# Four PSUM banks for the first feed-forward product, and a W2 ternary loop on DVE with four load buffers and two result buffers

## What is computed

```
def bitlinear(x, W, b):
    w_scale = jnp.clip(jnp.mean(jnp.abs(W)), EPS, None)
    Wq = _ste(W, jnp.clip(jnp.round(W / w_scale), -1.0, 1.0) * w_scale)
    x_scale = jnp.clip(jnp.max(jnp.abs(x), axis=-1, keepdims=True), EPS, None)
    xq = _ste(x, jnp.clip(jnp.round(x * (QB / x_scale)), -QB - 1.0, QB) * (x_scale / QB))
    return jnp.einsum('bnd,hd->bnh', xq, Wq) + b
h = bitlinear(x, W1, b1)          # 1024 -> 4096
h = jax.nn.gelu(h, approximate=False)
return bitlinear(h, W2, b2)       # 4096 -> 1024
```

## Time and profile before

| | |
|---|---|
| median of three runs | 3119.3 us |
| profiled execution, its own time | 3135.53 us |
| its span, slowest core (core 1) | 3133.9 us |
| spans of the eight cores | 3091.9 to 3133.9 us |
| busy PE, DVE, ACT, POOL | 986.5, 1412.7, 579.8, 253.8 us |
| mean granted TensorE clock | 0.65 of 2.4 GHz |

### The profile page before, as it was taken

One profiled execution on the slowest core, in us unless ns is written; L12 is line 12 of the kernel. 1 busy time (PEld: TensorE's weight loads), 2 busy tenths in 40 slices (PEclk: granted clock), 3 DMA queues, 4 the chain that ended last, 5 costly groups with the idle time before them and its releaser, 6 DMA issues.

```text
span 3133.9 us, 14949 instructions; the slowest of 8 cores (3091.9 to 3133.9 us)
## 1 busy us (share of the span) xinstructions
PE 986.5 (31%) x3428; PEld 350.8 (11%) x3428; DVE 1412.7 (45%) x1172; ACT 579.8 (19%) x476; POOL 253.8 (8%) x196
## 2 busy tenths in 40 slices
PE   2752334633321000766662001101001010126644
PEld 0100111211100000222221000000000000002211
DVE  1000324345345677445543225676676767740011
ACT  0213224324432110222221002010101011000000
POOL 0000000000000000222222440000000000000000
PEclk9875667766665555777776555555555555559878
DMA  6754010100000000222212441101101010138766
GB/s 232 273 183 159 14 40 21 41 20 20 20 27 0 0 0 8 86 74 80 75 60 88 121 120 54 67 34 47 54 33 67 34 67 34 47 114 285 257 215 215
DMA packets 70696, 265.47 MB, mean 85 GB/s; under 512 B 7504, under 2 KB 7888, under 8 KB 64208
## 3 DMA queue, kind: packets, MB, share of 16 engines
q1 hardware_dynamic: 35744, 155.20, 14.4%
q0 software_dynamic: 18304, 67.12, 6.1%
q10 hardware_dynamic: 16560, 42.19, 4.2%
HBM read 214.15 MB, written 50.33 MB: 84 GB/s over the span
## 4 chain that ended last, share of the span: by engine, by line
DVE 41%; DMA 19%; PE 18%; ACT 10%; issue 7%; POOL 3%; DVEq 1%; SPq 1%; ACTq 1%; POOLq 0%
DVE X L100 17%; DVE Hh L100 10%; DVE SC L100 8%; DMA RB<-w2qsp 6%; PE PB L1066 6%; PE PB L734 5%; ACT SC L100 3%; DMA SC<-w2T 3%; PE PB L1265 2%; ACT X L100 2%; PE PB L1305 2%; POOL X L100 2%; DMA M<-w2qsp 2%; DVE M L100 2%; DMA w2qsp<-X 2%
## 5 line engine op out<-in xcount | busy, mean ns | idle before, releaser
L100 DVE TENSOR_TENSOR SC<-PB,BS 128x512 f32<-128x512 f32 x160 | 110.7, 692 | 432.2 <-PE PB L1305 243.5
L734 PE MATMUL PB<-Hh,WSB 128*128 128x512 bf16 x768 | 194.6, 421 | 243.6 <-POOLq L56 130.8
L1066 PE MATMUL PB<-Hh,W1Q 128*128 128x512 bf16 x512 | 150.1, 462 | 289.9 <-POOLq L56 223.4
L100 DVE TENSOR_TENSOR X<-X 128x2048 bf16<-128x2048 bf16 (+1 forms) x120 | 206.8, 1723 | 14.8 <-PE PB L527 1.6
L1265 PE MATMUL PB<-Hh,M 128*128 128x512 bf16 x128 | 47.3, 550 | 396.1 <-DVEq L56 396.1
L1066 PE MATMUL PB<-Hh,RB 128*128 128x512 bf16 x512 | 144.1, 448 | 68.7 <-DVEq L56 68.7
L100 ACT ACTIVATE X<-X 128x4096 bf16<-128x4096 bf16 (+1 forms) x24 | 73.1, 3048 | 493.4 <-DVEq L56 492.4
L1265 PE MATMUL PB<-X,RB 128*128 128x512 bf16 x128 | 47.4, 551 | 368.9 <-DVEq L56 368.9
L100 DVE TENSOR_SCALAR X<-X 128x2048 bf16<-128x2048 bf16 (+1 forms) x145 | 139.0, 959 | 53.3 <-ACTq L56 35.7
L100 ACT ACTIVATE X<-SC,CPF 128x512 bf16<-128x512 f32 x128 | 92.4, 722 | 328.7 <-DVEq L56 328.2
L1305 PE MATMUL PB<-X,M 128*128 128x512 bf16 x384 | 97.7, 403 | 115.8 <-DMA M<-w2qsp 115.6
(11 more groups left out here) (168 smaller groups left out, 1571.6 us busy)
## 6 DMA issues: line engine op xcount, KB each, us to landing
X<-h1qsp SPq DMA_DIRECT2D x96, 512.0 KB, 6.4
SC<-w1T POOLq DMA_DIRECT2D x32, 512.0 KB, 7.4
WSTG<-w1T SPq DMA_DIRECT2D x32, 512.0 KB, 4.0
h1sp<-X POOLq DMA_DIRECT2D x32, 512.0 KB, 3.0
WSTG<-w2T SPq DMA_DIRECT2D x8, 2048.0 KB, 9.1
WSTG<-wmodT SPq DMA_DIRECT2D x6, 2048.0 KB, 9.5
SC<-wmodT SPq DMA_DIRECT2D x12, 1024.0 KB, 8.9
M<-w2qsp ACTq DMA_DIRECT2D x48, 256.0 KB, 7.3
```

What stands on the lines that cost most here:

```text
L100: ins = f(*a, **k)
L734: E.matmul(PB[pp + gi][:, :], WSB[:, gi * 1024 + k * 128: gi * 1024 + (k + 1) * 128], ntile(Hh, k, j), start=(k == 0), stop=(k == KC - 1)),
L1066: E.matmul(PB[jp][:, :], w1q[hc % 4][:, k * 128:(k + 1) * 128], ntile(Hh, k, j), start=(k == 0), stop=(k == KC - 1)),
```

## The change

Two edits. In the first feed-forward product the bank becomes `(hc * NNT + j) % 4`, and a product waits for the eviction four back. The W2 stretch is written anew: 16 units of half a slice, four load buffers with a semaphore each, comparisons into the bf16 tiles `W1Q` and `RB`, the subtraction on DVE, and the result in one of two halves of `X[:, 4096:12288]`, of which slice `s` takes the half that slice `s - 2` had, after waiting for that write. The write stays on POOL's queue and goes by turns on two semaphores.

```diff
--- before.py
+++ after.py
@@ -1052,7 +1052,7 @@
         if hc + 2 < HC:
             emit_tern(hc + 2)
         for j in range(NNT):
-            jp = j % 2
+            jp = (hc * NNT + j) % 4
             gidx = hc * NNT + j
             for k in range(KC):
                 wv = []
@@ -1060,8 +1060,8 @@
                     wv = [tern_dvs[hc]]
                     if gidx == 0:
                         wv += [("sDV", xq_done)]
-                    if gidx >= 2:
-                        wv += [("sDV", ffn1_evacs[gidx - 2])]
+                    if gidx >= 4:
+                        wv += [("sDV", ffn1_evacs[gidx - 4])]
                 p.on("tensor", lambda E, hc=hc, j=j, k=k, jp=jp:
                      E.matmul(PB[jp][:, :],
                               w1q[hc % 4][:, k * 128:(k + 1) * 128],
@@ -1113,40 +1113,47 @@
         inc=("sDV", 1))
     pl_m1h = ("sDV", p.cnt["sDV"])
 
-    w2stage = WSTG[:, 0:4096]
-    for s in range(KC):
-        wv = [("sSPa", p.cnt["sSPa"]), ("sSPb", p.cnt["sSPb"])] if s == 0 \
-            else [("sDV", p.cnt["sDV"])]
-        p.on("sync", lambda E, s=s: E.dma_start(out=w2stage, in_=w2T[s]),
-             wait=wv, inc=("sW2", 16))
-        w2n = p.cnt["sW2"]
-
-        def tern2a(E, s=s):
-            E.tensor_scalar(SC[1][:, 0:2048], w2stage[:, 0:2048],
-                            WS2i[:, 0:1], 0.5, ALU.mult, ALU.is_ge)
-            return E.tensor_scalar(SC[2][:, 0:2048], w2stage[:, 0:2048],
-                                   WS2n[:, 0:1], 0.5, ALU.mult, ALU.is_ge)
-        p.on("vector", tern2a,
-             wait=[("sW2", w2n)] + ([("sSP", p.cnt["sSP"])] if s >= 1 else []),
-             inc=("sDV", 1))
-        p.on("gpsimd", lambda E: E.tensor_tensor(
-            TRN2A, SC[1][:, 0:2048], SC[2][:, 0:2048], ALU.subtract),
-            wait=[("sDV", p.cnt["sDV"])], inc=("sPL", 1))
-
-        def tern2b(E, s=s):
-            E.tensor_scalar(SC[1][:, 0:2048], w2stage[:, 2048:4096],
-                            WS2i[:, 0:1], 0.5, ALU.mult, ALU.is_ge)
-            return E.tensor_scalar(SC[2][:, 0:2048], w2stage[:, 2048:4096],
-                                   WS2n[:, 0:1], 0.5, ALU.mult, ALU.is_ge)
-        p.on("vector", tern2b, wait=[("sPL", p.cnt["sPL"])], inc=("sDV", 1))
-        p.on("gpsimd", lambda E: E.tensor_tensor(
-            TRN2B, SC[1][:, 0:2048], SC[2][:, 0:2048], ALU.subtract),
-            wait=[("sDV", p.cnt["sDV"])], inc=("sPL", 1))
-        dvn = ("sPL", p.cnt["sPL"])
-        p.on("gpsimd", lambda E, s=s: E.dma_start(
-            out=w2qsp[:, :, s * 128:(s + 1) * 128].rearrange("k p c -> p k c"),
-            in_=X[:, 4096:8192].rearrange("p (k c) -> p k c", k=HC)),
-            wait=[dvn], inc=("sSP", 16), dma=True)
+    w2stg4 = [SC[1][:], SC[2][:], SC[3][:], WSTG[:, 0:2048]]
+    w2sem4 = ["sW2", "sW2b", "sW2c", "sW2d"]
+    w2u_dv = {}
+    w2spl = {}
+    for u in range(2 * KC):
+        s, h = u // 2, u % 2
+        st = u % 4
+        if u < 4:
+            wv = [("sSPa", p.cnt["sSPa"]), ("sSPb", p.cnt["sSPb"])]
+        else:
+            wv = [("sDV", w2u_dv[u - 4])]
+        sw = w2sem4[st]
+        p.on("sync", lambda E, s=s, h=h, st=st: E.dma_start(
+            out=w2stg4[st], in_=w2T[s][:, h * 2048:(h + 1) * 2048]),
+            wait=wv, inc=(sw, 16))
+        w2n = p.cnt[sw]
+
+        ioff = 4096 + (s % 2) * 4096
+
+        def tern2(E, st=st, h=h, ioff=ioff):
+            E.tensor_scalar(W1Q[:], w2stg4[st], WS2i[:, 0:1], 0.5,
+                            ALU.mult, ALU.is_ge)
+            E.tensor_scalar(RB[:], w2stg4[st], WS2n[:, 0:1], 0.5,
+                            ALU.mult, ALU.is_ge)
+            return E.tensor_tensor(
+                X[:, ioff + h * 2048:ioff + (h + 1) * 2048],
+                W1Q[:], RB[:], ALU.subtract)
+        tv = [(sw, w2n)]
+        if h == 0 and s >= 2:
+            tv += [w2spl[s - 2]]
+        p.on("vector", tern2, wait=tv, inc=("sDV", 1))
+        w2u_dv[u] = p.cnt["sDV"]
+        if h == 1:
+            ssp_s = "sSP" if s % 2 == 0 else "sSPa"
+            p.on("gpsimd", lambda E, s=s, ioff=ioff: E.dma_start(
+                out=w2qsp[:, :, s * 128:(s + 1) * 128].rearrange(
+                    "k p c -> p k c"),
+                in_=X[:, ioff:ioff + 4096].rearrange("p (k c) -> p k c",
+                                                     k=HC)),
+                wait=[("sDV", w2u_dv[u])], inc=(ssp_s, 16), dma=True)
+            w2spl[s] = (ssp_s, p.cnt[ssp_s])
     sp_all = p.cnt["sSP"]
 
     stmh_done = make_scales(STMH, [pl_m1h])
```

## The result

The changed kernel takes 2900.9 us in the median of 8 runs (2897.55 to 2905.59), beside 3120.4 for the kernel before. The ratio is 0.9292, 95% interval 0.9277 to 0.9307. The forecast was 2895. The profiled execution has a span of 2900.4 us on its slowest core, core 0; the cores lie between 2877.2 and 2900.4.

What follows compares the result with a forecast made beforehand. The prediction found no full engine, only stages in a row, with PE and DVE taking turns and W2 slices unoverlapped. Savings of 113.5 + 111.0 = 224.5 us from 3119.3 gave 2895 us, range 2875 to 2925 (64%).

Steps and rivals of the forecast that it cites:

- Part 1: First feed-forward product: four PSUM banks in place of two cut a step from 13.67 to 9.92 us, saving 113.5 us.
- Part 2: W2 stretch and the cast behind it: subtraction on DVE, more buffers; saves 106.7 plus 4.3 us, together 111.0.
- The law for a slice: W2 stretch: with two result halves, a slice takes max(8.7, (W + 8.7)/2) us.
- W: W2 stretch: time a write takes from the end of its slice; before the change 8.3 us plus 0.4 for the issue.
- the 10.8: W2 stretch: DMA time per slice, read 5.96 plus write 4.85 us, taken as bound of the six slices awaiting a write.
- The comparison: W2 stretch: DVE comparison writing bf16 from f32, a form not in the trace, taken to cost 1.29 us.
- The rival with 2.35: W2 stretch: comparisons run at the slow rate, 2.35 us instead of 1.29; slice 13.0 us, time 2917; chance 7%.
- The starved issue: W2 stretch: DVE's comparisons keep POOL from issuing writes until DVE stands; W 17.0, stretch 99.5 us, time 2907; chance 20%.
- The clock: First product: PE falls to 1.2 GHz for whole steps, 32 matmuls up to 14.5 us; time 2951 to 3008; chance 8%.
- even 8.52 fits under 9.92: First product: 32 matmuls, part of them slow, take 8.52 us and still fit beneath DVE's 9.92 us step.
- Slower: W2 stretch: reads beside writes make W so long that two halves of X fail; W = 100 gives 3157 us; chance 1%.
- The sum: Whole kernel: 113.5 + 111.0 = 224.5 us saved, giving 2895 us.

Runs made afterwards that it cites:

- the third buffer: The changed kernel with three result buffers in X for W2, so slice s waits for write s-3: 2900.75 us, ratio 0.9287; run again, 2898.0 us.
- three-bank kernel: The changed kernel with three PSUM banks instead of four and a wait for the eviction three back: 2903.3 us in one run.

## Why the prediction was right, point by point

**Part 1** was forecast to save 113.5 us and saved 431.0 - 319.4 = 111.6; alone, 111.3 in the time of the kernel. The step was forecast at 9.92 and is 9.95, the last two at 15.82 and are 15.77. The sum of DVE's distances was the right tool, since DVE has hardly anybody to wait for but Gelu: on core 0 two of 128 evictions wait noticeably for PE, 1.03 and 0.46 us. Of the 29 steps 21 are 9.89 to 9.91 us, the first is 8.83 and seven are 10.11 to 10.43, for instance when an eviction comes 0.35 us late; together that makes the 0.03.

**Part 2** was forecast to save 106.7 in the stretch and 4.3 in the cast. It saved 190.6 - 90.0 = 100.6 and 4.4 (from the cast to the next stage's first read it was 40.65 us and is 36.2). The step of it that was mis-sized is the stretch, 87.2 us forecast and 92.3 on core 0. Two terms make up the 5.1. The first load landed at 7.26 instead of 5.0, with three others issued beside it: 2.3. And the six slices behind the first two took 11.3 us each and not 10.8: 1573.74 + 17.4 to 1658.78 is 67.6, against 64.8, which is 2.8. DVE stood 13.5 us for writes in them, 2.2 per slice, about as forecast.

The law for a slice, (W + 8.7)/2, only says how the waits are chained, and they are: DVE ended slice 0 at 1582.1 and began slice 2 at 1596.39, so W = 14.3, and half of 14.3 + 8.7 is 11.5; measured 22.65 / 2 = 11.3 from start to start. The reason I gave for the 10.8 is wrong, and that the number came so near is in part luck. I took the DMA engines as the bound, with 10.8 us of their time per slice. They were at 0.82, and their time per slice was 54.0% x 92.3 / 8 + 28.3% x 92.3 / 7 = 6.2 + 3.7 = 10.0 us. With the third buffer a slice took 9.6 us on core 4, so 10.8 is no bound. What decides with two buffers is how long one write takes among the reads, and every second slice waits for it: 13.5 us of landing and 0.7 in front of its issue. That W grows because of the reads is shown by leaving them out.

**The comparison** that writes bf16 from f32 takes 1.286 us, the value chosen. The rival with 2.35 is out.

**The starved issue.** DVE and POOL do hold each other up: an issue beside comparisons takes 2.3 us instead of 1.7, and one comparison 2.23 instead of 1.29. But POOL is not kept waiting until DVE stands: its first issue ended at 1585.03, while DVE ran without a pause to 1591.7. W was 14.3 at that write, between the 12.9 behind the forecast (2 x 10.8 - 8.7) and the 17.0 of this rival, and so was the stretch, 92.3 between 87.2 and 99.5. What made it longer was the reads, not the issue: without reads writes land in 8.1 to 9.2 us beside the same comparisons. The rule of the Trainium skill ("SBUF — State Buffer", section "SBUF: two separate sides"), that GpSimd can't write descriptors during such a DVE operation, agrees in kind with these two numbers. Its advice, to issue from ACT or SP so that DVE and the DMA don't meet, took the stretched comparisons away here and cost 8 us in the stretch and 17 in the time.

**The clock** did not fall for whole steps, but it did for parts of eight: 0.94 was granted in the stretch. After an idle of 2.84 us 32 matmuls took 7.07 us, which is the full 2.4 GHz, in most steps, and 8.37 to 8.75 in some. The forecast had the cover right, "even 8.52 fits under 9.92": no step of core 0 is longer for it. The three-bank kernel shows what it costs where the cover is thinner.

**Slower** had nothing for it: the longest landing on any core was 16.2 us, far from 88.

**The sum.** 111.6 + 100.6 + 4.4 = 216.6 of the 219.5 us. The other 3 are not accounted for; they are within what the untouched stages differ from run to run; the first pass of the second product alone was 852 us in the mean before and 848 after. The forecast was 5.9 us too low: 1.9 in part 1 (1.4 of them because the profiled slowest core had a longer product than the others, 432.4 against 431.0), 6.1 in the stretch (5.1 from its length on the slowest core, the rest because the other cores had less to save), 1.1 because the kernel before ran at 3120.4 beside it and not at 3119.3, and 3 the other way that I had not forecast. One sum of a rival is off by 1: at W = 100 the kernel would take 3156 us, not 3157.

## What to carry to other kernels

Where two engines hand work to and fro, add up the distances from start to start on one of them as if it never waited for the other: if the other's work fits beneath, that sum is the new step. Read how many buffers are needed from it as well: here the third bank brought nearly everything, and the fourth only what covers PE's slow matmuls. With two buffers behind a slow write, a slice costs half of the write's landing plus the work, so price the landing under the traffic that the faster stage will make, not under today's.

## What the runs showed of the hardware

A DMA of 256-byte pieces from SBUF to DRAM is 1904 packets for 7.34 MB from POOL's queue and 28784 from ACT's. With no reads beside it, such a write of 1 MB lands in 6.2 us from ACT and 8.1 to 9.2 from POOL, but beside reads in 13.0 against 10.7 us (median of the first seven writes over all cores). An issue by POOL (1.7 us) and a DVE comparison of f32 (1.29 us) side by side each lose something, 0.6 and 0.94 us. The time of the DMA engines for the same write fell from 4.85 us to 3.7 when reads ran beside it, while that of a 2 MB read rose only from 5.96 to 6.2, so the sum of a quiet stretch, 10.8, overstated what the busy one needed, 10.0. A semaphore wait on DVE that is already met costs about 0.07 us (gaps of 0.27, 0.33 and 0.40 us). After the same idle of 2.84 us, PE's 32 matmuls took 7.07 us in some steps and up to 8.75 in others.
